# First attention of a two-layer gated cross-attention network: raw transposed rows times mean-free folded keys, the scores scaled afterwards

## The reference, cut to what matters

```
x = x + tanh(g_xattn[0]) * L0_xattn(layernorm(x), ctx, ctx)   # one head, no scale, no output projection
x = x + tanh(g_ffn[0])   * L0_ffn(layernorm(x))               # 256 -> 1024 -> 256, piecewise gelu on a grid
x = x + tanh(g_xattn[1]) * L1_xattn(layernorm(x), ctx, ctx)   # 16 heads
x = x + tanh(g_ffn[1])   * L1_ffn(layernorm(x))               # 8 experts, top two
L0_xattn: softmax((xn Wq + bq) (ctx Wk + bk)^T) (ctx Wv + bv),   xn = (x - mean) / sqrt(var + eps)
```

## Time and profile before

| | us |
|---|---|
| median of 3 runs | 490.95 (490.82 to 492.32) |
| profiled execution | 491.95 |
| its span on the core | 490.2 |
| first feed-forward matmul starts | 41.21 |
| TensorE busy | 454.8 (93% of the span) |
| VectorE busy | 370.4 (76%) |
| ScalarE busy | 258.6 (53%) |
| POOL busy | 145.6 (30%) |

### The profile page before, as it was taken

The page is one execution under the profiler, slowest core; times in us unless marked ns, Lnnn a source line. Parts: engine busy times, 40 slices in busy tenths (PEclk is TensorE's granted clock), DMA queues, the critical chain, the costliest instruction groups (busy, mean ns, idle before and its releaser), DMA issues.

```text
span 490.2 us, 8549 instructions
## 1 busy us (share of the span) xinstructions
PE 454.8 (93%) x3226; PEld 395.9 (81%) x3226; DVE 370.4 (76%) x753; ACT 258.6 (53%) x416; POOL 145.6 (30%) x122
## 2 busy tenths in 40 slices
PE   6999999999998999998997499999999999999991
PEld 4787789798887888787886259989999999999991
DVE  4689998898988978899898966686757475757441
ACT  2577899697965664556554132463434344442220
POOL 3354100010002211222113063215263645445153
PEclk9999999999999999999999799999999999999997
DMA  7412200000000101312123341134363747461031
GB/s 243 136 43 60 82 1 2 0 1 1 1 0 1 45 1 44 117 57 87 45 86 127 126 125 55 23 130 136 98 162 96 170 96 195 86 174 20 3 48 16
DMA packets 37135, 36.06 MB, mean 74 GB/s; under 512 B 6442, under 2 KB 35942, under 8 KB 36966
## 3 DMA queue, kind: packets, MB, share of 16 engines
q1 hardware_dynamic: 30633, 27.65, 17.3%
q0 software_dynamic: 6144, 7.66, 9.1%
q10 hardware_dynamic: 317, 0.21, 0.1%
HBM read 27.69 MB, written 8.39 MB: 74 GB/s over the span
## 4 chain that ended last, share of the span: by engine, by line
PE 75%; DVE 15%; issue 4%; DMA 2%; ACT 1%; POOL 1%; ACTq 0%; DVEq 0%; POOLq 0%
PE PS L1489 19%; PE PS L1490 18%; PE PS L1491 18%; PE PS L1898 5%; PE PS L1509 2%; DVE nmaxC L1181 2%; PE PS L1844 2%; PE PS L1909 2%; DVE xn L1020 1%; DVE tmp L1184 1%; DVE st L993 1%; DMA tmp<-in_L_xattn_Wk 1%; PE PS L1546 1%; PE PS L1760 1%; DVE tmp L1231 1%
## 5 line engine op out<-in xcount | busy, mean ns | idle before, releaser
L1489 PE MATMUL PS<-w_hi,hT_hi 128*128 128x256 f32 x384 | 110.3, 287 | 0.8 <-DVE hT_lo L1161 0.6
L1490 PE MATMUL PS<-w_lo,hT_hi 128*128 128x256 f32 x384 | 108.6, 283 | 0.0
L1491 PE MATMUL PS<-w_hi,hT_lo 128*128 128x256 f32 x384 | 108.6, 283 | 0.0
L964 ACT ACTIVATE tmp<-PS,biasT 128x512 f32<-128x512 f32 (+1 forms) x80 | 43.8, 600 | 111.1 <-PE PS L1491 111.1
L673 POOL DMA_INDIRECT out<-tmp,dst_idx x32 | 56.1, 1754 | 98.6 <-DVE tmp L1445 91.8
L1489 PE MATMUL PS<-xT_hi,w_hi 128*128 128x512 f32 (+1 forms) x224 | 81.6, 364 | 1.1 <-DVE xT_lo L1028 1.1
L1490 PE MATMUL PS<-xT_lo,w_hi 128*128 128x512 f32 (+1 forms) x224 | 80.8, 361 | 0.0
L1491 PE MATMUL PS<-xT_hi,w_lo 128*128 128x512 f32 (+1 forms) x224 | 80.4, 359 | 0.0
L1489 PEld LDWEIGHTS PS<-w_hi,hT_hi 128*128 128x128 f32 x384 | 73.4, 191 | 4.1 <-issue 2.2
L1490 PEld LDWEIGHTS PS<-w_lo,hT_hi 128*128 128x128 f32 x384 | 73.5, 191 | 0.8
L1491 PEld LDWEIGHTS PS<-w_hi,hT_lo 128*128 128x128 f32 x384 | 73.5, 191 | 0.0
(11 more groups left out here) (254 smaller groups left out, 819.9 us busy)
## 6 DMA issues: line engine op xcount, KB each, us to landing
w_raw<-in_L_ffn_w SPq DMA_DIRECT2D x72, 256.0 KB, 3.0
residual<-in_x SPq DMA_DIRECT2D x4, 512.0 KB, 5.3
out<-residual SPq DMA_DIRECT2D x3, 512.0 KB, 4.2
normed_rows<-xn SPq DMA_DIRECT2D x3, 512.0 KB, 3.6
kv<-in_L_ffn_b SPq DMA_DIRECT2D x1, 1024.0 KB, 6.5
tmp<-in_L_xattn_Wq SPq DMA_DIRECT2D x2, 256.0 KB, 5.4
out<-residual SPq DMA_DIRECT2D x2, 256.0 KB, 4.2
normed_rows<-xn SPq DMA_DIRECT2D x2, 256.0 KB, 3.1
```

Of the source, the lines that this page charges most:

```text
L964: act.activation(gD[:, G % 2, f, 0:P * n], H[:, G % 2, f, 0:P * n], ACT.Gelu, bias=biasT[:, col:col + 1]).then_inc(e_gelu, 1)
L1489: pe.matmul(o, lh, rh, start=start, stop=False, skip_group_check=skip)
L1490: pe.matmul(o, lh, rl, start=False, stop=False, skip_group_check=skip)
L1491: return pe.matmul(o, ll, rh, start=False, stop=stop, skip_group_check=skip)
```

## The change

The host lays out five inputs anew: x also transposed (xT), the context transposed, Wq0 and Wo1 transposed, and all bias vectors as columns. The turns of the setup and the copies behind them go; Wo1's turn in output_bias goes too.

The scores are now raw transposed rows times KW. For that Wq0's transposed rows are made mean-free on VectorE (centre_queries), which takes the row mean out of the product; 1/sqrt(var + eps) and beta are put on afterwards, by one scale-and-add on VectorE per tile, from the accumulators into a buffer sA in which the exponentials are taken in place. So chunks 0 to 3 are no longer normalised, turned and copied; their xT chunks, four more loads of 512 KB, come straight from the host's array. Wk1, Wv1, Wv0, bv0 and the gates are now loaded from ScalarE's queue. On TensorE the second layer's keys and both value products stand ahead of the first scores. The warming matmuls in the setup go. wq_lo moves from VectorE to POOL and wq_hi to ScalarE; high_parts(3) moves into the feed-forward's step 0; statistics of round NC + 1 move behind x_lo(NC). The late weights wait on SP for the scores of three chunks.

```diff
@@ SP
-            load_x(0), Wq0, load_x(1), Wv1, Wv0, bv0, gates, load_x(2), Wk1, biases, load_x(3)
...
             def load_x(c):
+                sp.dma_start(xT_raw(c), xT.rearrange("(k p) n -> p k n", p=P)[:, :, 512 * c:512 * c + 512]).then_inc(xT_loaded[c], 16)
                 sp.dma_start(xr[:, 4 * c:4 * c + 4, :], xf[:, 4 * c:4 * c + 4, :]).then_inc(x_loaded[c], 16)
+            sp.dma_start(wqT, WqT0.rearrange("(k p) d -> p k d", p=P)).then_inc(wq0_loaded, 16)
             load_x(0)
             load_x(1)
             load_x(2)
             load_unit(0)
+            load_x(3)
             load_unit(1)
             for dst, src in ((wq1_raw, Wq1), (wg_raw[:, :, :], wg)):
...
+            sp.wait_ge(a_scores, 3)
             for dst, src in ((wo[:, :, 0:D], Wo1.rearrange("(k p) e -> p k e", p=P)),
+                             (woT, WoT1.rearrange("(a p) r -> p a r", p=P)),
...
@@ POOL
-            power(0)
-            power(1)
-            pool.wait_ge(xn_ready, 2)
             pool.memset(Vblk[:, :, :, 0:P], 0.0).then_inc(vblk_zeroed, 1)
-            power(2)
-            for c in range(1, NC):
-                pool.wait_ge(a_scores, c + 1)
-                low_parts(c - 1, 0, 1)
-                power(c + 2)
-                low_parts(c - 1, 1, 2)
-            pool.wait_ge(knot_ready, 1)
-            low_parts(NC - 1)
+            for c in range(NC):
+                power(c)
+            low_parts(0, 0, 1)
+            power(NC)
+            low_parts(0, 1, 2)
+            low_parts(1)
+            pool.wait_ge(wq_rounded, 1)
+            pool.tensor_tensor(wq_lo[:, :, :], wq1_raw, wq_hi[:, :, :].bitcast(F32), ALU.subtract).then_inc(wq_split, 1)
+            low_parts(2)
+            power(NC + 1)
+            low_parts(3)
             power(NC + 2)
@@ ScalarE
+            act.dma_start(ctxT, ctxT_in).then_inc(ctx_loaded, 16)
             act.dma_start(wk0_sb, Wk0).then_inc(ctx_loaded, 16)
+            act.dma_start(biasT[:, :], bias_columns).then_inc(bias_loaded, 16)
+            act.dma_start(wk1_sb, Wk1).then_inc(setup_loaded, 16)
+            act.dma_start(wv1_sb, Wv1).then_inc(v1_loaded, 16)
+            for dst, src in ((wv0_sb, Wv0), (bv0_row[0:1, :], bv0.rearrange("(r p) -> r p", r=1)),
+                             (gates[:, 0:2], g_xattn.partition_broadcast(P)), (gates[:, 2:4], g_ffn.partition_broadcast(P))):
+                act.dma_start(dst, src).then_inc(v0_loaded, 16)
...
+                    act.activation(sA[:, c % 2, i, :], sA[:, c % 2, i, :], ACT.Exp, bias=soft[:, c % 2, 0, i:i + 1],
                                    accum_out=soft[:, c % 2, 1, i:i + 1]).then_inc(a_exp, 1)
...
+            exponentials(0)
+            copy_turned(0)
+            exponentials(1)
+            exponentials(2)
+            copy_turned(1)
+            high_parts(0)
+            high_parts(1)
+            copy_turned(2)
+            act.wait_ge(query_loaded, 32)
+            act.activation(wq_hi[:, :, :], wq1_raw, ACT.Copy).then_inc(wq_rounded, 1)
+            exponentials(3)
+            x_hi(NC)
+            act.activation(small[:, 20:21], small[:, 16:17], ACT.Gelu)
+            copy_turned(3)
+            high_parts(2)
+            act.wait_ge(wq_split, 1)
...
                     if g + 1 < NB_PAIRS:
                         to_grid(g + 1)
+                    if g == 0:
+                        high_parts(PAIRS - 1)
@@ VectorE
+            def centre_queries():
+                dve.wait_ge(wq0_loaded, 16)
+                for k in range(KD):
+                    ins = dve.bn_stats(wq_stats[:, k, :], wqT[:, k, :])
+                link(ins)
+                for k in range(KD):
+                    ins = dve.bn_aggr(wq_mean[:, k, :], wq_stats[:, k, :])
+                link(ins)
+                for k in range(KD):
+                    ins = dve.tensor_scalar(wqT[:, k, :], wqT[:, k, :], wq_mean[:, k, 0:1], None, ALU.subtract)
+                ins.then_inc(wq_centred, 1)
...
+            def largest(c):
                 dve.wait_ge(a_scores, c + 1)
+                dve.wait_ge(rstd_ready, c + 1)
+                dve.wait_ge(kw_copied, 2)
                 if c >= 2:
+                    dve.wait_ge(a_tr, c - 1)
+                for i in range(4):
+                    dve.scalar_tensor_tensor(out=sA[:, c % 2, i, :], in0=SA[c % 2][:, i, :], scalar=rstd[:, c, i:i + 1],
+                                             in1=beta[:, c // (NC // 2), :], op0=ALU.mult, op1=ALU.add).then_inc(a_shift, 1)
+                dve.wait_ge(a_shift, 4 * (c + 1))
+                dve.tensor_reduce(soft[:, c % 2, 0, :], sA[:, c % 2, :, :], AX_X, ALU.max, negate=True).then_inc(a_max, 1)
...
+            largest(0)
+            stats(2)
+            largest(1)
+            stats(3)
+            invert(0)
+            largest(2)
+            invert(1)
+            attended(0)
+            stats(NC)
+            largest(3)
+            apply(NC)
+            attended(1)
+            invert(2)
             x_lo(NC)
+            attended(2)
+            invert(3)
+            stats(NC + 1)
             dve.wait_ge(tanh_ready, 1)
             output_units()
+            apply(NC + 1)
@@ TensorE
             keep_warm(4, 6)
+            pe.wait_ge(ctx_loaded, 16 * N_CTX)
+            keys(4, wk0_sb)
+            pe.wait_ge(setup_loaded, 16)
+            keys(5, wk1_sb)
+            pe.wait_ge(bias_loaded, 16)
             pe.wait_ge(kt_copied, 1)
             for k in range(KD):
+                ins = pe.matmul(PS[:, 3, 0:2 * KEYS], bcast(biasT[:, BQ0 + k:BQ0 + k + 1], [P, P]), KT0[:, k, :],
+                                start=(k == 0), stop=(k == KD - 1))
+            ins.then_inc(kw_psum, 1)
+            pe.wait_ge(wq_centred, 1)
...
+            pe.wait_ge(v1_loaded, 16)
...
+            pe.wait_ge(v0_loaded, 16 * N_V0)
...
             def attend_scores(c):
+                pe.wait_ge(xT_loaded[c], 16)
...
+                        ins = pe.matmul(SA[c % 2][:, i, :], xT_raw(c)[:, k, P * i:P * i + P],
+                                        KW[:, k, b, :], start=(k == 0), stop=(k == KD - 1))
...
             attend_scores(0)
+            attend_scores(1)
+            attend_turn(0)
+            attend_scores(2)
+            attend_values(0)
+            attend_turn(1)
+            attend_scores(3)
+            attend_values(1)
+            attend_turn(2)
+            transpose_x(NC)
+            attend_values(2)
+            attend_turn(3)
-            for c in range(1, NC):
-                attend_scores(c)
-                transpose_x(c + 1)
-                attend_values(c - 1)
-                attend_turn(c)
```

More of the change, by code:

```diff
@@ L169, in flamingo_gated_two_layers @@
         ctxT = take(0, 2, KEYS)
-        xT_odd = take(1, KD, 512)
+        xT_third = take(1, KD, 512)
         V1 = take(1, 2, D)
-        eA = take(1, 4, KEYS)
+        sA = take(1, 2, 4, KEYS)
+        beta = take(1, 2, KEYS)
         KW = take(1, KD, 2, KEYS)
-        wv1_sb = take(1, D)
-        bv0_row = take(1, D)
+        wv1_sb = take(0, D)
+        bv0_row = take(0, D)
         bo_row = bo_bc[:, 0:D]
@@ L277, in flamingo_gated_two_layers @@
         wq0_loaded = sem("wq0_loaded")
-        b0_loaded = sem("b0_loaded")
+        bias_loaded = sem("bias_loaded")
+        xT_loaded = [sem(f"xT_loaded{c}") for c in range(NC)]
+        wq_centred = sem("wq_centred")
+        keys_psum = sem("keys_psum")
+        kw_psum = sem("kw_psum")
+        v0_psum = sem("v0_psum")
+        a_shift = sem("a_shift")
+        wq_rounded = sem("wq_rounded")
+        wq_split = sem("wq_split")
         v0_loaded = sem("v0_loaded")
@@ L466, in _ @@
         def _(sp):
-            def later(dst, src):
-                sp.dma_start(dst, src).then_inc(setup_loaded, 16)
             def load_x(c):
+                sp.dma_start(xT_raw(c), xT.rearrange("(k p) n -> p k n", p=P)[:, :, 512 * c:512 * c + 512]).then_inc(xT_loaded[c], 16)
                 sp.dma_start(xr[:, 4 * c:4 * c + 4, :], xf[:, 4 * c:4 * c + 4, :]).then_inc(x_loaded[c], 16)
[L473 to L477, removed]
+            sp.dma_start(wqT, WqT0.rearrange("(k p) d -> p k d", p=P)).then_inc(wq0_loaded, 16)
             load_x(0)
-            sp.dma_start(wq0_sb, Wq0.rearrange("(k p) e -> p k e", p=P)).then_inc(wq0_loaded, 16)
             load_x(1)
[L482 to L486, removed]
-            load_x(2)
[L488 to L492, removed]
-            load_x(3)
+            load_x(2)
             def load_unit(u):
@@ L792, in _, with copy_turned @@
-            for c in range(NC):
-                exponentials(c)
-                if c + 1 < NC:
-                    x_copy(c + 1)
-                else:
-                    x_hi(NC)
-                    act.activation(small[:, 20:21], small[:, 16:17], ACT.Gelu)
-                if c == 0:
-                    first_values()
+            def copy_turned(c):
                 act.wait_ge(a_tr, c + 1)
```

(14 more changed lines are left out.)

245 lines of the change are left out of this document (72 added, 173 removed).

## The result

The changed kernel took 498.97 us (median of four runs, 497.66 to 500.71), the kernel before 490.88 (490.72 to 492.32): ratio 1.016, 95% interval 1.0118 to 1.0203. It is slower, by 8.1 us, where 4.5 less was forecast. Its four runs come in two pairs, near 497.8 and near 500.4; the profiled one is of the first (497.66, span 495.9). Between the profiled executions of the two kernels the loss is 5.7 us (497.66 against 491.95).

What follows compares the result with a forecast made beforehand. Bound by TensorE's order behind loads, then VectorE's order with hand-overs to TensorE and ScalarE. Terms -0.3 + 4.9 + 0.5 - 0.6 = 4.5 us saved, so a median of 486.45; range 484.4 to 489.5.

Steps and rivals of the forecast that it cites:

- Term D: POOL beside VectorE: apply(4) runs beside low_parts(0) and takes near 1.8 us; minus 0.6 us, no other instructions charged.
- the port rule: VectorE and GpSimd hold a shared port for whole instructions; POOL's 6.0 us before the feed-forward lost, giving 491.85.
- the short form: The skill's sentence under "Terms": the shared port is held for a whole instruction and the loser fully blocks; 491.85.
- rival 4: Setup loads: ScalarE's small broadcast loads land last, so V0 and all scores wait; 492.55, chance 0.06.
- Rival 2: TensorE's clock falls while it waits for apply(4)'s rows, or rises late at the start; 488.35, chance 0.22.
- Term C: Feed-forward: four weight turns leave output_bias, plus 0.5 us; first low half ends 3.1 earlier, cover of 1.1 us left.
- Term A: Start to end of first scores: removed turns replaced by products put in front, scores end at 18.3; minus 0.3 us.
- order of issue: Setup loads: transfers land in the order issued over both queues, so Wk1 lands at 8.3.
- rival 1: Setup loads: queues share the engines, second keys start at 8.1, scores end 0.6 earlier; 485.8, chance 0.15.
- Term B: First scores to feed-forward: VectorE's shorter order lets hidden(0) start at 36.5, 18.2 us against 23.2; plus 4.9 us.
- rival 3: VectorE's scale-and-adds cost 0.41 us each, 3.6 us more over four calls; 490.05, chance 0.06.
- the wait of 0.4 for POOL's power: Before apply(4): power(4), queued behind half of low_parts(0), ends at 31.2, while VectorE would have asked at 31.0.

Runs made afterwards that it cites:

- e6: e5 with ScalarE forming high parts 0 and 1 one step earlier, so GpSimd subtracts beside VectorE's scale-and-add, statistics and residual; 491.18 us.
- e4: The changed kernel with 24 warming products without use on TensorE ahead of the turn of round 4; 498.57 us.
- e1: The changed kernel with GpSimd waiting until apply(4) is done before its remaining subtractions; 495.71 us.
- e2: The changed kernel with statistics of round 5 moved ahead of the low half of round 4 on VectorE; 500.12 us.
- e5: The changed kernel with the moves of e1, e2 and e3 together, and round 5's power ahead of low parts 1 and 2 on GpSimd; 497.51 us.
- e7: e6 with 16 warming products without use in three TensorE gaps of the attention loop; 490.76 us.
- e3: The changed kernel with high_parts(3) back ahead of the feed-forward's loop and low_parts(3) back behind its first segment; 496.17 us.
- e9: e7 with high part 2 formed earlier on ScalarE and low part 2 subtracted on GpSimd once round 5's variances stand; 489.6 us.
- e10: e9 with the scores of chunk 0 ahead of both value products on TensorE; 488.89 us.
- e12: e10 with V1's products kept ahead of the scores of chunk 0 and only V0's behind; 488.05 us, 0.9948 of the kernel before.
- e8: The changed kernel with GpSimd's subtractions for pairs 0 to 3 cut into instructions of 128 columns, nothing moved; 498.52 us.
- e11: The changed kernel with 16 warming products in three gaps of the attention loop; 499.82 us.

## Why the prediction was wrong

**Term D failed, by its mechanism.** "apply(4) near 1.8 us" was 5.17, and "I charge no others" was false for the statistics' last step (0.79 and 0.98 in place of 0.17), and for the uint16 product (3.28 in place of 1.22). Held time of VectorE: 3.8 + 0.6 + 0.8 + 2.1 = 7.3 us, where 0.6 was charged. The trace of the kernel before had shown the sign. In the row of 1.81 us, from which I took the 0.6, one tile takes 0.91 and ends at 30.33, a subtraction at 30.17; the other three take 0.40. So the price there was for a subtraction met, not for a normalisation. And a row of four columns took 0.48 in place of 0.17, to the end of the subtraction beside it; VectorE, then GpSimd, both of the kernel before:

```profile
27.36 0.48 DVE L1004 TENSOR_SCALAR ve<-mv 128x4 f32<-128x4 f32 x1
```

```profile
26.56 1.26 POOL L599 TENSOR_TENSOR w_lo<-w_raw,w_hi 128x512 fp32r<-128x512 f32 x1 [6.19 <-ACT w_hi L728]
```

I set the port rule aside because "the residual updates do not bear it out for operations of two inputs". They could not have: they read one operand from the accumulators. The Trainium skill, "SBUF — State Buffer", section "Who interferes with whom", says which VectorE instructions contend with GpSimd: copies, casts and tensor-by-scalar operations in the mode that uses two ports, and those with two inputs in SBUF while GpSimd reads SBUF; reductions and those with at most one SBUF input outside that mode do not. Every row here agrees: held were tensor-by-scalar (128x256 and 128x4), the casts, and the uint16 product; free were the residual update, the subtraction from the accumulators, the scale-and-add and the maximum. I had weighed the sentence under "Terms" without this list, and taken as evidence an instruction that the list exempts. By the charge worked out from the short form the time would have been 491.85, nearer and still 7 short: it stopped at the end of the second stretch. The forecast left it no more than 0.01 ("slower 0.07" less rival 4's 0.06), though its 491.85 lies among the times called the same.

**Rival 2 was named, and the clock fell in another place.** It fell at 31.5 us, while TensorE was at work, before the 5.96 us that the lock made. TensorE had idled twice ahead of it, 1.24 us to 22.03 and 1.18 us to 29.57. The lock is not needed for it: in e6, where apply(4) takes 1.37, the clock was low from 29.7 to 36.5. The turn lost 0.9 us by it; with the clock held up (e4) 0.4 came back. In e1, e2 and e5 it falls already at 22.6 to 22.8, within 0.1 us of the end of the first of these idle times. If the higher runs are of this kind, which their mean clocks suggest, that costs 2.6 us between the changed kernel's pairs and 4.7 between e5's. The change itself had opened that idle time: four warming products stood ahead of attend_turn(0), and it took them out. (The six at 3.3 us stayed, other than "The change" has it.) e7 puts four back there and twelve elsewhere, the idle time is 0.38, and none of its ten runs shows the fall. Which of the three places does it was not tried, and e4, with both idle times, kept its clock: what decides stays open.

**Term C failed in its cover.** I let the first low half end only 3.1 us earlier than before and still took 4.5, as TensorE was to ask for it 1.1 later. No such cover exists: from the start of that low half to the end of the span it is 430.7 us in the changed kernel, e2, e3, e6, e7, e9, e10 and e12, 430.8 in e4 and 430.9 before, while the start itself lies anywhere from 55.37 to 68.18. VectorE, busy 22.3 of 23.3 us there, is what the end follows: TensorE's first product of these hidden columns stands 2.8 us behind the start of that low half in the changed kernel (68.08) and 5.2 in the one before (64.47), and the end keeps its distance all the same. By its own numbers the forecast should have been 3.1 at most, not 4.5. Where the span behind the low half is longer (e1, e5, e8, e11: 432.2 to 433.5), the clock fell once more behind 60 us: from 77 to 81 us in e1 and e11, from 63.7 to 70.6 in e5, from 62.4 to 65.8 in e8, there beside the late pieces of pair 3. Falls at 67.1 to 70.5 in e2 and 63.1 to 66.5 in e4 cost nothing. The stretch itself, from the start of hidden(0) to the end of that low half, took 23.45 us (43.01 to 66.46) for 20.9; 2.1 of the 2.5 are the held product. Statistics 5, which I blamed for the narrow cover, gave nothing back when moved (e2).

**Term A was 0.7 off.** First scores ended at 19.02, forecast 18.3. In the chain of waits the second layer's key weights, Wk1, landed 1.35 later than by order of issue:

```profile
2.30 7.35 DMA tmp<-in_L_xattn_Wk
```

so neither order of issue (8.3) nor rival 1 (8.1) holds for it. That V0 followed V1 at once was right. e12 shows what I had not asked: the products of V0 need not stand ahead of the first scores (1.55 us between e9 and e12).

**Term B was right but for D and the clock.** The scale-and-adds took 0.91 for four against 0.78 forecast (1.25 less the maximum's 0.47), far from rival 3. The line through the two rows gives 0.185 us for 77 columns, not the 0.22 that I read from it; one took 0.29, and 0.23 in a row. In e12, without locks and fall, hidden(0) starts at 37.34 (forecast 36.5), the first low half ends at 56.59 (57.4), and the profiled execution takes 487.90 (487.45). It starts its loop 1.9 us earlier than the changed kernel, so the agreement is partly luck. hidden(0) in the changed kernel is 6.5 late: 0.7 from A, 0.6 the held statistics, 0.4 the four calls of largest, 3.9 apply(4) (5.17 for the 1.3 by which 36.5 was worked out), 0.9 the turn at 1.2 GHz. These make 6.5; but the wait of 0.4 for POOL's power, which was counted in, did not come, so that 0.4 has no name. With 2.5 in the feed-forward and 1.4 of cover that was not there, less 0.3 for the stretch behind (430.66 us against 430.93), that makes 10.1 of the 10.2 us between 487.45 and the profiled 497.66. A last slip: I subtracted from the median of the kernel before a saving that was measured against its profiled execution. That one was 1.0 us longer than the median, and e12's profiled execution is not longer than its own (487.90 against 488.05). So a saving of 4.1 between the two profiles is 2.7 between the medians. Where the profiled execution of the kernel before lost its 1.0 us is open. The lower end of the range, too, adds up to 484.9 by its own terms (485.8 less 0.3 and 0.6) and not to 484.6; nothing hangs on it.

## What to carry to other kernels

Before work goes to GpSimd, list what VectorE does in the same microseconds, and sort it by operands. In these traces tensor-by-scalar operations and casts within SBUF (the on-chip memory), and operations with two SBUF inputs, wait out GpSimd's whole instruction, while those with an operand in the accumulators, statistics and reductions pass; so did a tensor-by-scalar operation of a single column (0.15 us in e2). Place GpSimd's long instructions beside the second kind; cutting them (e8) only changed who waits. Where a wait is moved, look for the row that it lands on: e5 and e6 freed apply(4) and held the casts. An instruction that was not held up is evidence only for instructions with the same places of operands.

## What the runs showed of the hardware

- VectorE and GpSimd hold each other up in both directions and instruction by instruction: one tile of 256 columns took 2.43 us, the length of GpSimd's 1024-column subtraction (2.37 to 2.41 us); GpSimd's eight short pieces took 6.53 us beside VectorE's products and 3.74 at 43.45. It is not only subtractions: two tensor-by-scalar operations of 256 columns (centre_queries) took 1.99 us beside the zeroing of 2.23 us on GpSimd at 4.49, off the path.
- A wait of 0.61 us on TensorE near 14 us preceded a stretch at half speed up to 27 us in e10 (two products of Wv 1.99 us against 1.09 in e12), while the granted clock of these rows reads 1.00. With that wait filled by work that was needed anyway (e12), none of five runs is of the second kind, against four of ten. Chance alone would give that about one time in thirteen, so that the wait brings it on is likely and not shown. In the kernel before too, products ran at the lower level below a recorded 1.00, so that durations, not the column, tell the clock there.
